# A state space layer's side work in other banks and steps, two more sums on ScalarE and GpSimd, and a convolution's first term on ScalarE

## The chip, the cores and the metric

The kernel runs on one core of a Trainium2 chip. The metric is the time of one execution on the device, in microseconds (us). A core has five engines that run their own programs side by side and meet at semaphores: TensorE (PE), VectorE (DVE), ScalarE (ACT), GpSimd (POOL) and SyncE (SP), which here only starts transfers. PE writes to PSUM, which the kernel uses as eight banks of 512 float32 per partition; ScalarE and VectorE read it.

## What is computed

Four residual layers on x (4 images, 384 channels, 48 by 48 positions). Only the first, a state space (Mamba) block, is touched by the change. The other three (a patch-wise Fourier filter, a deformable 11 by 11 depthwise convolution, a mixture of four experts) follow it in time.

```python
xs = gn(x).transpose(0, 2, 3, 1).reshape(b, L, c)          # L = 2304
xin, z = split(xs @ in_proj_w.T)                           # 768 channels each
xc = conv1d(xin, conv_w, taps=4, causal, per channel)
xin = silu(xc + conv_b)
dt, B, C = split(xin @ x_proj_w.T, [24, 16, 16])
dt = softplus(dt @ dt_proj_w.T + dt_proj_b)
for t in range(L):                                         # h: 768 x 16
    h = exp(dt[t] * A) * h + dt[t] * B[t] * xin[t]
    y[t] = sum over the 16 states of h * C[t]
y = (y + xin * D) * silu(z)
out = layernorm(y @ out_proj_w.T) * ln_gamma + ln_beta
x = x + out
```

## The kernel before

The sequence of an image (2304 positions) is cut into NQ = 6 chunks of T = 384 positions; four images give NCH = 24 chunks, `k`. A chunk is worked off in STEPS = 96 steps, `n`, that is 48 pairs of steps: 16 states, and for each three pairs of channel blocks.

The main work of a pair `p`: ACT makes two exps of dt times A (L600) and sets the start state (L605), seven steps ahead; POOL makes dt * x * B for a state, transposed, into `a_dBT` (L882); PE transposes it into the PSUM tensor `pw0` or `pw1` (`inputs`, L451, at even steps); DVE runs the recurrence as one scan over two channel blocks (L744). Then PE turns one third of the state's result into `pw2` (`turned`, L462, at odd steps), and DVE multiplies it by C and adds it to the accumulator `a_acc` (`weighed`, L763; L757 for the first state). That is a unit `u`, 48 in a chunk; the unit of pair `p` is `p - 3`. `pw2` holds one unit at a time, so `turned` waits until the unit before is read. The units in LENT (20, 22, 24, 26, 38, 41, 43) don't go to DVE: ACT copies them with the factor C to `a_tm12` (L614) and POOL adds them (L894). `lent(hh)` counts them, for the values that the semaphores `a_cw`, `p_cw`, `v_acc` are waited for.

The side work is one chunk behind or ahead. For chunk k-1 (`post_*`): skip term and gate (transposes A, L344; DVE L640; POOL L793), the output projection O (L353), layer norm (ACT L490, DVE L646, POOL L799 to L803, ACT L493), transposes G (L360), DVE L655, and the store. For chunk k+1 (`pre_*`, `gate_*`): the input projection P (L373), its copy to `a_raw` (L509), the convolution of four taps (first term on POOL, L828; three products on ACT, L521; three sums on POOL, L834), one Silu over the chunk (L524), and one over the gate (L567), the x projection X (L381), B and C turned (L387), the dt projection V (L394) with Abs and Relu (L548, L549), Exp and Ln (L552, L556) for the softplus, POOL L841 and L845, transposes T (L401) with ACT L562, and the gate projection Z (L413) with ACT L577.

The order is written by hand: each of these generators yields the step at which its next piece is due, and `march` merges them, on each engine for itself, by due time: at step `n` all pieces due by `n` come first, then the main work. PE takes side pieces at odd steps only (`odd=True`), ahead of `turned`. The due times are the tables A_AT, O_AT, LN_AT, G_AT, T_AT, Z_AT and the numbers in the yields. The engines' programs are fixed in this order, and each instruction waits for those ahead of it.

The side groups use two PSUM banks of one bank each: `ps3` (S) and `ps2` (D). `Turn.claim` keeps them in turn: a group that takes a bank waits for the semaphore with which the one before it there was read. P, the turned B and C, V, T and Z are in S; A, O, X, G and the statistics in D.

In the third chunk of an image (q = 2) the next image's group norm statistics are gathered: SP loads 18 pieces to `a_sx` (`stats`, L951), one after the other, and DVE reads each (L705). SP also loads `a_xs` for chunk k+2 (L946) and stores chunk k-1 (`store0`, L926), in one queue.

Of the kernel before, what the change touches and what calls it, by code (L numbers as in the profile page):

```python
# [323 lines left out]

# [1857 lines left out]
```

## Time and profile before

| | us |
|---|---|
| median of 3 runs | 5354.77 |
| lowest and highest | 5343.97, 5362.83 |
| the profiled execution | 5347.93 |
| its span, first to last instruction | 5346.1 |
| state space layer, scans from and to | 126.1, 3328.9 |
| an ordinary chunk | 133.0 |
| a chunk with statistics | 144.2 |

The span is that of the profiled execution; 1.8 us of its time lie around it. The times of an engine's groups of instructions are sums of their durations; where instructions overlap, start to start is shorter than the mean duration. In the timelines, the number in brackets is the idle time of the engine before the instruction and what ended it. The chunk that starts at 1055.6 us (the eighth) is taken as the ordinary one; step n of it is reached by DVE with its scan number n/2.

### The profile page before, as it was taken

What the parts mean: (1) busy time and instruction counts of PE and PEld (TensorE: products, weight loads), DVE (VectorE), ACT (ScalarE), POOL (GpSimd) and SP (SyncE); (2) the same over time, 40 slices, a digit from 0 to 9 for tenths busy, and PEclk for the clock granted to TensorE, in tenths of its full rate; (3) what the DMA queues carried; (4) which work ended last, traced back from release to release, by engine and by line L of the source; (5) the groups of instructions that cost most, each with busy time, mean ns of one, the idle gap of its engine ahead of it and who ended that gap; (6) DMA issues with size and microseconds to landing.
All of it is one profiled execution on the core that took longest, in us unless ns stands there. A gap on an engine that the chain in (4) does not pass through costs nothing.

```text
span 5346.1 us, 78656 instructions
## 1 busy us (share of the span) xinstructions
PE 4686.3 (88%) x28623; PEld 3835.5 (72%) x28623; DVE 4381.3 (82%) x4965; ACT 3070.4 (57%) x6391; POOL 2970.7 (56%) x3552
## 2 busy tenths in 40 slices
PE   4888888888888888888888886779998899999999
PEld 2666666666666666666666665446877799999999
DVE  1999999999999999999999999677677765665555
ACT  3777777777777777777777774333332223333333
POOL 3776777777777777777777775456554520000000
PEclk8999999999999999999999999889797988999999
DMA  2001000001000001000000001110201021112110
GB/s 78 1 13 33 10 10 10 10 11 35 10 10 10 10 11 35 10 10 10 10 10 10 10 5 44 44 32 20 92 20 41 26 72 53 54 51 60 45 60 29
DMA packets 96933, 148.64 MB, mean 28 GB/s; under 512 B 5748, under 2 KB 93604, under 8 KB 96548
## 3 DMA queue, kind: packets, MB, share of 16 engines
q1 hardware_dynamic: 96548, 143.63, 8.4%
q8 instruction: 227, 3.72, 0.3%
q14 instruction: 158, 1.29, 0.1%
HBM read 101.00 MB, written 42.61 MB: 27 GB/s over the span
## 4 chain that ended last, share of the span: by engine, by line
PE 50%; issue 15%; DVE 15%; POOL 12%; ACT 7%; DMA 1%; POOLq 0%; DVEq 0%; SPq 0%; ACTq 0%
PE pw L1776 8%; PE pw L1763 6%; PE pw L462 6%; PE pw L451 6%; DVE a_h L744 5%; POOL a_dBT L882 4%; PE ps L413 3%; PE ps L353 3%; DVE b_cv L1393 3%; PE ps L373 2%; DVE a_acc L763 2%; PE ps L1763 2%; POOL a_xin L834 2%; POOL a_acc L894 2%; PE pw L1176 2%
## 5 line engine op out<-in xcount | busy, mean ns | idle before, releaser
L744 DVE TENSOR_TENSOR_SCAN a_h<-a_dA,pw 128x771 f32<-128x771 f32 x1152 | 2015.7, 1752 | 125.6 <-PE pw L451 124.6
L600 ACT ACTIVATE a_dA<-a_dt,a_Aneg 128x384 f32<-128x384 f32 x2304 | 1345.5, 607 | 155.0 <-DVE a_h L744 150.1
L462 PEld LDWEIGHTS pw<-g_ident,a_h 128*128 128x128 f32 x6912 | 786.6, 142 | 619.8 <-DVE a_acc L763 267.1
L882 POOL TENSOR_SCALAR a_dBT<-a_dtxT,a_BC 128x768 f32<-128x768 f32 x1152 | 1026.2, 909 | 300.7 <-PE pw L451 216.6
L462 PE MATMUL pw<-g_ident,a_h 128*128 128x128 f32 x6912 | 983.1, 279 | 227.5 <-DVE a_acc L763 158.1
L451 PE MATMUL pw<-g_ident,a_dBT 128*128 128x128 f32 x6912 | 958.9, 276 | 4.8 <-POOL a_dBT L882 4.8
L763 DVE SCALAR_TENSOR_TENSOR a_acc<-pw,a_BC,a_acc 128x768 f32<-128x768 f32 x912 | 915.3, 1004 | 52.5 <-PE pw L462 48.1
L451 PEld LDWEIGHTS pw<-g_ident,a_dBT 128*128 128x128 f32 x6912 | 806.5, 143 | 6.5 <-POOL a_dBT L882 5.5
L834 POOL TENSOR_TENSOR a_xin<-a_xin,a_tm 128x384 f32<-128x384 f32 x432 | 433.3, 1003 | 34.2 <-ACT a_tm L521 9.0
L1887 DVE TENSOR_TENSOR d_hf<-d_hf,d_wb 128x384 f32<-128x384 f32 x288 | 159.1, 557 | 312.4 <-ACT d_hf L1819 300.2
L894 POOL TENSOR_TENSOR a_acc<-a_acc,a_tm 128x768 f32<-128x768 f32 x168 | 307.4, 1830 | 171.1 <-ACT a_tm L614 170.2
L413 PE MATMUL ps<-a_xn,a_WinT 128*128 128x384 f32 x864 | 345.5, 502 | 30.7 <-ACT a_sz L577 15.1
L373 PE MATMUL ps<-a_xn,a_WinT 128*128 128x384 f32 x864 | 350.8, 490 | 10.2 <-ACT a_raw L509 5.1
L353 PE MATMUL ps<-a_WoT,a_sz 128*128 128x384 f32 x864 | 338.9, 489 | 23.1 <-POOL a_sz L793 23.1
L1819 ACT ACTIVATE d_hf<-pw,d_b 128x384 f32<-128x384 f32 x216 | 125.2, 580 | 352.0 <-PE pw L1763 352.0
L1279 ACT ACTIVATE b_xh<-ps 128x384 fp32r<-128x384 f32 x144 | 70.6, 490 | 415.5 <-PE ps L1132 415.5
L1776 PE MATMUL pw<-e_hh,c_W2h 128*128 128x384 f32 x864 | 288.8, 334 | 1.7 <-DVE e_hl L1892 1.7
L1776 PE MATMUL pw<-e_hl,c_W2h 128*128 128x384 f32 x864 | 288.6, 334 | 0.0
L1776 PE MATMUL pw<-e_hh,c_W2l 128*128 128x384 f32 x864 | 288.6, 334 | 0.0
L1591 POOL TENSOR_SCALAR b_xw<-b_x,b_sw,b_bw 128x384 f32<-128x384 f32 x288 | 223.1, 796 | 114.8 <-PE pw L1132 114.7
L1575 POOL TENSOR_TENSOR b_cv<-b_cv,b_tm 128x768 f32<-128x768 f32 x96 | 196.3, 2045 | 131.4 <-ACT b_tm L1260 127.0
L521 ACT ACTIVATE a_tm<-a_raw,a_pv 128x384 f32<-128x384 f32 x432 | 259.5, 601 | 7.4 <-POOL a_xin L834 7.3
(228 smaller groups left out, 9377.7 us busy)
## 6 DMA issues: line engine op xcount, KB each, us to landing
d_wb<-cw SPq DMA_DIRECT2D x24, 768.0 KB, 5.7
a_xs<-in_x SPq DMA_DIRECT2D x24, 576.0 KB, 3.9
x<-a_xs SPq DMA_DIRECT2D x24, 576.0 KB, 3.0
b_x<-x SPq DMA_DIRECT2D x24, 576.0 KB, 4.4
b_xs<-x SPq DMA_DIRECT2D x24, 576.0 KB, 5.0
e_xs<-x SPq DMA_DIRECT2D x24, 576.0 KB, 3.8
out<-e_xs SPq DMA_DIRECT2D x24, 576.0 KB, 5.8
a_sx<-in_x SPq DMA_DIRECT2D x54, 192.0 KB, 2.3
```

Of the source, the lines that this page charges most:

```text
L353: t = e.matmul(pd[:, 0:C], m[f"a_sz{o}"][:, j, tb * 128:(tb + 1) * 128], m["a_WoT"][:, j, :], start=j == 0, stop=j == 5)
L373: t = e.matmul(ps[:, 0:T], m["a_WinT"][:, kk, i * 128:(i + 1) * 128], m["a_xn"][:, kk, :], start=kk == 0, stop=kk == 2)
L413: t = e.matmul(ps[:, 0:T], m["a_WinT"][:, kk, DI + i * 128:DI + (i + 1) * 128], m["a_xn"][:, kk, :], start=kk == 0, stop=kk == 2)
L451: t = e.transpose(ps[:, at:at + 128], m[f"a_dBT{g % 2}"][:, tb, (c + h) * 128:(c + h + 1) * 128], ident[:])
L462: t = e.transpose(m["pw2"][:, c * 128:(c + 1) * 128], m[f"a_h{g % 2}"][:, c // 2, first_col(c) + tb * 128:first_col(c) + (tb + 1) * 128], ...
L600: e.activation(dA[:, first_col(c):first_col(c) + T], m[f"a_dt{k % 2}"][:, c, :], ACT.Exp, scale=m["a_Aneg"][:, c, n:n + 1]).then_inc(s["a_ ...
L744: e.tensor_tensor_scan(m[f"a_h{g % 2}"][:, p % 3, :], m[f"a_dA{pi % NDA}"][:], m[f"pw{pi % 2}"][:, COL:COL + PAIR], 1.0, ALU.mult, ALU.add ...
L763: e.scalar_tensor_tensor(out=acc, in0=ps, scalar=cs, in1=acc, op0=ALU.mult, op1=ALU.add).then_inc(s["v_acc"], 1)
L834: e.tensor_tensor(xin[:, i, :], xin[:, i, :], m[f"a_tm{pr % NTM}"][:], ALU.add).then_inc(s["p_cv"], 1)
L882: t = e.tensor_scalar(m[f"a_dBT{g % 2}"][:, tb, :], m[f"a_dtxT{o}"][:, tb, :], m[f"a_BC{o}"][:, tb, n:n + 1], 1.0, ALU.mult, ALU.mult)
L1763: t = e.matmul(hidden3(m, hi), m[f"c_{A}"][:, kk, col], m[f"e_{B}{o}"][:, kk, :], start=kk == z == 0, stop=kk == z == 2)
L1776: t = e.matmul(ps, m[f"c_{A}"][:, i, col], m[f"e_{B}{u % 2}"][:, i, :], start=x == 0 and i == 0 and z == 0, stop=x == 3 and i == z == 2, s ...
```

## The change

- Units 6 and 13 (EARLY) go to ACT and POOL as well, in all chunks but those with statistics, so nine of 48 in 21 chunks. They use a new buffer, `a_tm13`, that lies over `a_sx` and `a_dt3`, with the waits that this needs.
- The first term of the convolution goes from POOL (L828) to ACT (`a_c0`), in the order first, second, third, fourth tap, for the first block second, third, first, fourth.
- V alternates between the banks S and D, T goes from S to D.
- Other due times: O and the layer norm earlier, X, B and C, V, Exp and Ln later, G from 60, 62.5, 66 to 68.1, 72.1, 76.1, Z and T other steps, Z with spacing 1.2 for 1.3.
- SP starts 16 instead of 13 of the statistics' loads ahead of the store of chunk k-1 and the load of chunk k+2.

```diff
-    m.new("a_sx", [128, T])
...
+    at = m.at
+    m.new("a_tm13", [128, DI])
+    m.section(at)
+    m.new("a_sx", [128, T])
     m.new("a_dt3", [128, T], F32R)
...
-O_AT, O_GAP, LN_AT = (18.8, 30, 40.2), (1.8, 1.6, 1.1), (29.5, 39.8, 47)
-G_AT = (60, 62.5, 66)
-T_AT = (78.6, 79.8, 81, 85.6, 86.6, 87.6)
-Z_AT = (63.5, 67.5, 71.5, 75, 82, 88.8)
+O_AT, O_GAP, LN_AT = (18.4, 29.2, 39.2), (1.8, 1.6, 1.1), (29.1, 39, 46.3)
+V_AT = (58.4, 59.5, 60.6, 61.7, 62.8, 63.9)
+G_AT = (68.1, 72.1, 76.1)
+T_AT = (80.2, 81.1, 82, 86, 86.9, 87.8)
+Z_AT = (64.8, 68.8, 72.8, 76.8, 82.8, 89.6)
+Z_GAP = 1.2
-LENT = (20, 22, 24, 26, 38, 41, 43)
+LENT, EARLY = (20, 22, 24, 26, 38, 41, 43), (6, 13)
+def has_stats(k):
+    return k % NQ == 2 and k // NQ + 1 < NB
+def lent_units(k):
+    return () if k == NCH else LENT if has_stats(k) else EARLY + LENT
...
@@ pre_pe
-        yield 47 + 1.2 * j
+        yield 47.7 + 1.2 * j
-    yield 56.8
+    yield 57.4
-        yield 58 + 0.8 * i
-        S.claim("a_v", 6 * k + i + 1)
+        yield V_AT[i]
+        (D if i % 2 else S).claim("a_v", 6 * k + i + 1)
-            S.claim("a_dtx", 6 * k + 3 * hf + tb + 1)
+            D.claim("a_dtx", 6 * k + 3 * hf + tb + 1)
@@ gate_pe
-            yield at + 1.3 * kk
+            yield at + Z_GAP * kk
@@ pre_act
-        for j in range(1, 4):
-            yield 6.2 + 5.4 * i + j
+        for j in (1, 2, 0, 3) if i == 0 else (0, 1, 2, 3):
+            yield 6.2 + 5.4 * i + 0.8 * j + (2 if i == 0 and j in (0, 3) else 0)
+            if j == 0:
+                w.wait_ge("p_sz", 6 * (k - 2) + i + 1)
+                w.wait_ge("p_dtx", 6 * (k - 1) + i + 1)
+                e.activation(m[f"a_xin{o}"][:, i, :], raw[:, i, 0:T], ACT.Identity, scale=pv[:, i, 0:1], bias=pv[:, i, 4:5]).then_inc(s["a_c0"], 1)
+                continue
-    yield 54.5
+    yield 55.2
-    yield 57.3
+    yield 57.9
-        yield 58.4 + 0.8 * i
+        yield V_AT[i] + 0.4
-    yield 64.5
+    yield 65.3
-    yield 67
+    yield 67.5
@@ gate_act
-        yield at + 3
+        yield at + 2 * Z_GAP + 0.4
@@ weighed on ACT
-        w.wait_ge("p_cv", 24 * min(k + 2, NCH))
+        if u in EARLY:
+            w.wait_ge("v_st", GN * min(k // NQ + (k % NQ > 2), NB - 1) + 18)
+            w.wait_ge("pe_V", 6 * (k + 1))
+        else:
+            w.wait_ge("p_cv", 18 * min(k + 2, NCH))
@@ pre_pool
-        yield 7.5 + 5.4 * i
...
-        e.tensor_scalar(xin[:, i, :], raw[:, i, 0:T], pv[:, i, 0:1], pv[:, i, 4:5], ALU.mult, ALU.add).then_inc(s["p_cv"], 1)
         for j in range(1, 4):
-            yield 7.5 + 5.4 * i + j
+            yield 7.5 + 5.4 * i + j + (1.5 if i == 0 else 0)
+            w.wait_ge("a_c0", 6 * k + i + 1)
@@ added on POOL
-        e.tensor_tensor(acc, acc, m["a_tm12"][:], ALU.add).then_inc(s["p_cw"], 1)
+        e.tensor_tensor(acc, acc, m["a_tm13" if u in EARLY else "a_tm12"][:], ALU.add).then_inc(s["p_cw"], 1)
@@ l0_sp
-        for i in range(more - 5):
+        for i in range(more - 2):
             stats(b + 1, i)
         if k > 0:
             store0(e, m, d, w, k - 1)
         if k + 2 < NCH:
             load(k + 2)
-        for i in range(max(0, more - 5), more):
+        for i in range(max(0, more - 2), more):
             stats(b + 1, i)
```

## Rows read from the trace of the kernel before

**Rows 1.** The page's first part: busy us of each engine, share, instructions.

```profile
PE 4686.3 (88%) x28623; PEld 3835.5 (72%) x28623; DVE 4381.3 (82%) x4965; ACT 3070.4 (57%) x6391; POOL 2970.7 (56%) x3552
```

**Rows 2.** Busy time by windows, three chunks: window, length, engines, PEclk, DMA, GB/s.

```profile
1055.60:1188.60 133.00, 116.49 (x750) 89.66 (x750) 126.31 (x107) 101.15 (x218) 101.47 (x128) 0.99 0.04 11
1467.30:1598.50 131.20, 114.82 (x750) 88.33 (x750) 126.08 (x106) 100.92 (x218) 101.22 (x127) 1.00 0.03 10
1188.60:1332.80 144.20, 120.69 (x750) 90.89 (x750) 135.08 (x130) 101.77 (x219) 101.87 (x128) 0.96 0.11 32
```

**Rows 3.** Groups of instructions by line: count, busy us, mean ns, idle before.

```profile
L763 DVE SCALAR_TENSOR_TENSOR a_acc<-pw,a_BC,a_acc 128x768 f32<-128x768 f32 x912 | 915.3, 1004 | 52.5 <-PE pw L462 48.1
...
L894 POOL TENSOR_TENSOR a_acc<-a_acc,a_tm 128x768 f32<-128x768 f32 x168 | 307.4, 1830 | 171.1 <-ACT a_tm L614 170.2
...
L614 ACT ACTIVATE a_tm<-pw,a_BC 128x768 f32<-128x768 f32 x168 | 151.2, 900 | 129.1 <-PE pw L462 129.1
...
L828 POOL TENSOR_SCALAR a_xin<-a_raw,a_pv 128x384 f32<-128x384 f32 x144 | 95.0, 660 | 30.4 <-ACT a_raw L509 25.7 <-POOL a_sz L793 4.6
```

**Rows 4.** Timeline of DVE, ordinary chunk: start, us, line; two scans in a row last.

```profile
1081.95 1.75 DVE L744 TENSOR_TENSOR_SCAN a_h<-a_dA,pw 128x771 f32<-128x771 f32 x1
...
1084.82 1.75 DVE L744 TENSOR_TENSOR_SCAN a_h<-a_dA,pw 128x771 f32<-128x771 f32 x1
...
1087.42 1.75 DVE L744 TENSOR_TENSOR_SCAN a_h<-a_dA,pw 128x771 f32<-128x771 f32 x1
...
1106.28 1.75 DVE L744 TENSOR_TENSOR_SCAN a_h<-a_dA,pw 128x771 f32<-128x771 f32 x1
...
1137.84 3.51 DVE L744 TENSOR_TENSOR_SCAN a_h<-a_dA,pw 128x771 f32<-128x771 f32 x2
```

**Rows 5.** Timeline of PE, ordinary chunk, steps 19 to 21.

```profile
1082.31 0.88 PE L353 MATMUL ps<-a_WoT,a_sz 128*128 128x384 f32 x2 [1.14 <-POOL a_sz L793]
1083.03 0.82 PE L462 MATMUL pw<-g_ident,a_h 128*128 128x128 f32 x6
...
1085.63 0.82 PE L462 MATMUL pw<-g_ident,a_h 128*128 128x128 f32 x6
```

**Rows 6.** Timeline of ACT, ordinary chunk, at step 34.

```profile
1102.09 0.49 ACT L509 ACTIVATE a_raw<-ps 128x384 f32<-128x384 f32 x1 [0.65 <-PE ps L373]
1103.04 0.71 ACT L493 ACTIVATE a_ob<-a_ob,a_lsc 128x384 f32<-128x384 f32 x1 [0.46 <-POOL a_lsc L803]
```

**Rows 7.** Timeline of all engines, ordinary chunk, Silu and steps 46 to 48.

```profile
1111.00 2.13 ACT L524 ACTIVATE a_xin<-a_xin 128x2304 f32<-128x2304 f32 x1
...
1121.51 0.91 PE L381 MATMUL ps<-a_xin,a_WxT 128*128 128x384 f32 x2 [2.00 <-ACT a_ob L490]
...
1124.81 1.76 DVE L744 TENSOR_TENSOR_SCAN a_h<-a_dA,pw 128x771 f32<-128x771 f32 x1 [2.54 <-PE pw L451]
```

**Rows 8.** The same, the dt matmuls, step 61.

```profile
1137.81 0.45 PE L394 MATMUL ps<-a_dt,a_Wdt 128*128 128x384 f32 x1 [1.14 <-ACT a_raw L549]
```

**Rows 9.** The same, from the x copy to the Ln, and step 90.

```profile
1131.86 0.47 ACT L532 ACTIVATE a_dt<-ps 128x384 fp32r<-128x384 f32 x1
...
1150.60 0.49 ACT L577 ACTIVATE a_sz<-ps 128x384 f32<-128x384 f32 x1
1150.98 2.21 ACT L556 ACTIVATE a_dt<-a_dt,a_one 128x2304 f32<-128x2304 f32 x1
...
1181.69 1.76 DVE L744 TENSOR_TENSOR_SCAN a_h<-a_dA,pw 128x771 f32<-128x771 f32 x1 [1.10 <-PE pw L451]
```

**Rows 10.** Timelines of SP and DVE in a chunk with statistics.

```profile
1286.51 0.38 SPq L926 DMA_DIRECT2D x<-a_xs  x1
...
1294.06 0.56 DVE L705 BATCH_NORM_STATS2 a_bn<-a_sx 128x6 f32<-128x384 f32 x1 [4.08 <-DMA a_sx<-in_x]
...
1304.95 1.02 DVE L763 SCALAR_TENSOR_TENSOR a_acc<-pw,a_BC,a_acc 128x768 f32<-128x768 f32 x1 [2.58 <-PE pw L462]
```

**Rows 11.** Busy time by windows, the stretch at low clock in the ordinary chunk.

```profile
1122.50:1125.90 3.40, 3.40 (x15) 2.69 (x14) 1.09 (x1) 2.37 (x5) 2.30 (x4) 0.50 0.02 5
```

More of the change, by code:

```diff
@@ L311, with is_lent @@
 A_AT = (6.2, 8, 9.8, 11.6, 13.4, 15.2)
-O_AT, O_GAP, LN_AT = (18.8, 30, 40.2), (1.8, 1.6, 1.1), (29.5, 39.8, 47)
-G_AT = (60, 62.5, 66)
-T_AT = (78.6, 79.8, 81, 85.6, 86.6, 87.6)
-Z_AT = (63.5, 67.5, 71.5, 75, 82, 88.8)
-LENT = (20, 22, 24, 26, 38, 41, 43)
+O_AT, O_GAP, LN_AT = (18.4, 29.2, 39.2), (1.8, 1.6, 1.1), (29.1, 39, 46.3)
[9 more added lines that the diff above has]
+    return () if k == NCH else LENT if has_stats(k) else EARLY + LENT
+def is_lent(hh):
+    return hh >= 0 and hh % PAIRS in lent_units(hh // PAIRS)
 def lent(hh):
-    k, u = divmod(hh, STEPS // 2)
-    return len(LENT) * k + sum(x < u for x in LENT)
+    k, u = divmod(hh, PAIRS)
+    return sum(len(lent_units(i)) for i in range(k)) + sum(x < u for x in lent_units(k))
 def chunk(k):
@@ L389, in pre_pe @@
     for i in range(6):
-        yield 58 + 0.8 * i
-        S.claim("a_v", 6 * k + i + 1)
+        yield V_AT[i]
+        (D if i % 2 else S).claim("a_v", 6 * k + i + 1)
         w.wait_ge("v_dt3", k + 1)
         w.wait_ge("v_w", 7)
-        e.matmul(ps[:, 0:T], m["a_Wdt3"][:, i * 128:(i + 1) * 128], m["a_dt3"][:], start=True, stop=True).then_inc(s["pe_V"], 1)
+        e.matmul((pd if i % 2 else ps)[:, 0:T], m["a_Wdt3"][:, i * 128:(i + 1) * 128], m["a_dt3"][:], start=True, stop=True).then_inc(s["pe_V"], 1)
     for hf in range(2):
@@ L456, in turned @@
         w.wait_ge("v_scan", 3 * g + 3)
-        if hh > 0 and (hh - 1) % PAIRS in LENT:
+        if is_lent(hh - 1):
             w.wait_ge("a_cw", lent(hh))
@@ L531, in pre_act @@
     w.wait_ge("pe_BC", k)
+    if k > 0:
+        w.wait_ge("p_cw", lent(PAIRS * (k - 1) + EARLY[-1] + 1))
     e.activation(m["a_dt3"][:], pd[:, 0:T], ACT.Copy).then_inc(s["a_x"], 1)
     e.activation(m["a_tm0"][32:64, :], pd[32:64, 0:T], ACT.Copy).then_inc(s["a_x"], 1)
-    yield 57.3
+    yield 57.9
     w.wait_ge("pe_BC", k + 1)
@@ L547, in pre_act @@
         w.wait_ge("a_exp", 3 * PAIRS * (k - 1))
-        e.activation(dt[:, i, :], ps[:, 0:T], ACT.Abs, bias=pv[:, i, 5:6])
-        e.activation(raw[:, i, 3:T + 3], ps[:, 0:T], ACT.Relu, bias=pv[:, i, 5:6]).then_inc(s["a_v"], 1)
-    yield 64.5
+        pi = pd if i % 2 else ps
+        e.activation(dt[:, i, :], pi[:, 0:T], ACT.Abs, bias=pv[:, i, 5:6])
+        e.activation(raw[:, i, 3:T + 3], pi[:, 0:T], ACT.Relu, bias=pv[:, i, 5:6]).then_inc(s["a_v"], 1)
+    yield 65.3
     w.wait_ge("a_v", 6 * (k + 1))
     e.activation(dt[:], dt[:], ACT.Exp, scale=-1.0).then_inc(s["a_sp"], 1)
-    yield 67
+    yield 67.5
     w.wait_ge("a_sp", 2 * k + 1)
@@ L561, in pre_act @@
         hf, tb = divmod(u, 3)
-        e.activation(m[f"a_dtxT{o}"][:, tb, hf * T:(hf + 1) * T], ps[:, 0:T], ACT.Copy).then_inc(s["a_dtx"], 1)
+        e.activation(m[f"a_dtxT{o}"][:, tb, hf * T:(hf + 1) * T], pd[:, 0:T], ACT.Copy).then_inc(s["a_dtx"], 1)
 def silu_gate(e, m, w, k):
@@ L623, in main @@
         def main(n):
-            if n % 2 == 0 and n // 2 - TB - 1 in LENT:
+            if n % 2 == 0 and n // 2 - TB - 1 in lent_units(k):
                 weighed(k, n // 2 - TB - 1)
@@ L660, in pre_dve @@
     s, ps, dt3 = m.s, m["ps2"], m["a_dt3"]
-    yield 55.3
+    yield 56
     w.wait_ge("pe_X", k + 1)
@@ L809, in halo_pool @@
     w.wait_ge("a_pr", 18 * k)
+    w.wait_ge("a_c0", 6 * k)
     if k % NQ == 0:
@@ L912, in main @@
         def main(n):
-            if n % 2 and (n - 3) // 2 - TB in LENT:
+            if n % 2 and (n - 3) // 2 - TB in lent_units(k):
                 added(k, (n - 3) // 2 - TB)
@@ L950, in stats @@
         w.wait_ge("v_st", GN * (b - 1) + 18 if i == 0 else GN * b + i)
+        w.wait_ge("p_cw", lent(PAIRS * (NQ * (b - 1) + 2)))
         e.dma_start(m["a_sx"][:], xv[b, :, c, q * T:(q + 1) * T]).then_inc(s["d_sx"], 16)
```

29 lines of the change are left out of this document (12 added, 17 removed).

## The prediction

> **What bounds the kernel now.** I read the busy times first, then the time by chunk, then the order of instructions inside one chunk. Over the whole span TensorE (PE) is busy 88% and VectorE (DVE) 82% [rows 1]. The change touches only the state space layer, 24 chunks that start between 126 and 3206 us. An ordinary chunk takes 133.0 us; DVE is busy for 126.3 of them, ScalarE (ACT) for 101.2, GpSimd (POOL) for 101.5 [rows 2]. A chunk in which the statistics of the next image are gathered takes 144.2 us with the TensorE clock at 0.96, and one whose clock never fell takes 131.2 us [rows 2].
>
> A DVE busy for 95% looks like the bound. It is only half of it. In the stretch of steps 19 to 38 a pair of steps takes 2.60 us on DVE, scan to scan [rows 4]. PE takes 2.60 us there too, from one turned sum to the next (1083.03 to 1085.63): six transposes of state, six of inputs, one projection matmul and one output matmul, 0.65 us each, no idle time between them; the first and the last are shown [rows 5]. Two engines run at the same pace, and work taken from one of them shortens nothing. Elsewhere DVE waits for PE: 2.54 us where the x projection begins, 1.10 at step 90; in the dt matmuls PE waits for each eviction [rows 7, 8, 9].
>
> **How I count.** Pair by pair, from those durations. A pair costs PE 1.30 us of transposes plus its side groups (0.65 for a 384-column matmul of two passes, 0.33 for three transposes). A turned sum may start once the sum before it is read, and DVE wants it 1.66 us later, at the end of its scan (a scan of 1.75 us, less the overlap); it takes PE 0.82 [rows 4, 5]. So PE may be 0.8 us late for nothing, and 2.60 - 1.30 = 1.3 us of side work a pair keep it from falling further behind. What goes beyond that, DVE waits for.
>
> **Part 1: two more units to ACT and POOL (6 and 13).** 21 chunks have them: not the three with statistics. A unit is a weighted sum of 1.00 us on DVE; ACT's copy takes 0.90 [rows 3]. What DVE gives up is less than the row's mean, since instructions overlap: two scans in a row take 3.51 us, so a pair without a sum takes 1.75 and the gain is 2.60 - 1.75 = 0.85 us, 1.7 for both [rows 4]. Both lie inside the PE-paced stretch.
> Unit 6 is turned at step 19. There PE waits until POOL has the last gated product: 1.14 us [rows 5]. POOL loses 2 x 0.66 us of convolution before it [rows 3], but must now wait for the third product from DVE, so I let it finish 0.3 us earlier. Yet the output matmul, due at 18.8 behind a projection matmul at 18.7, is now due at 18.4, before it, so 0.65 us of work falls behind the wait. PE leaves step 19 0.3 us later, and the unit gains nothing.
> Unit 13 is turned at step 33. ACT's program has, before that copy, the copy of the last projection, whose matmul stands in that same step of PE: then 0.5 us for it, 0.5 for the new first term, 0.6 for a layer norm scaling, 0.5 for a product [rows 3, 6]. The copy starts 2.1 us after ACT gets its first input, and PE's next turned sum waits about 1.4 us. The output matmuls also move forward: three instead of two groups in step 31, the first behind an ACT copy that now has a first term ahead of it, 0.4 us.
> Added up for steps 18 to 36: 24.3 us before (scans at 1081.95 and 1106.28, [rows 4]), 26.4 after, **+2.0 us** where the skipped sums promise -1.7: PE falls back 0.3 us at step 19, 0.4 at 31 and 1.4 at 33, and since PE paces these pairs, the two sums bring nothing.
>
> **Part 2: the first term of the convolution.** POOL loses 6 x 0.66 us and gains 2 x 1.83; ACT gains 6 x 0.5 and 2 x 0.9 [rows 3]. ACT idles 32 us of 133, most of it in steps 6 to 36 waiting for PE [rows 2, 6], which hides its 4.8. If that cover were gone, it would cost at most those 4.8 us a chunk. But the second added unit holds POOL's last convolution sums until the ACT copy is there, so Silu starts 3.2 us later than before (1111.0 [rows 7]), 1.2 us later against the scans.
>
> **Part 3: the other steps.** Before, the x projection waits until 1121.51 for an ACT copy and DVE's scan sits idle 2.54 us; PE then runs at clock 0.50 for 3.4 us [rows 7, 11]. A chunk without that drop is 1.8 us shorter (133.0 - 131.2 [rows 2]). After, the projection is due one pair later and the copy one exp sooner, but Silu is late. I get waits of 0.8 us for the layer norm statistics and 0.5 for a turned sum, in place of 3.2 (the 2.54, the sum before that waits too, and its aftermath): **-1.9 us** over steps 36 to 50, with no drop of the clock there.
> The dt matmuls alternate between two banks, which ends the wait of 1.14 us for each eviction [rows 8]. What is late next is ACT: a matmul pair every 2.6 us needs 1.9 us of Abs and Relu beside 1.1 us of exps, and at step 60 the lent copy 26 now stands behind a dt eviction whose matmul is in PE's step 61. Waits of 1.2, 0.6 and 0.2 us remain where, with the end of the x projection, about 2.6 stood. Steps 50 to 68: **-0.6 us**, besides 1.6 us of layer output work (G) that only moves to steps 69 to 77.
> Then a new wait. The first gate group's copy was due at 66.5, before the Ln at 67 (1150.60 and 1150.98, [rows 9]). It is now due at 67.6, behind the Ln at 67.5. The second gate group starts in the same step of PE (69) in which the first ends, and needs that copy. From the x copy (1131.86) to the Ln ACT took 19.1 us; I find 18.5 after, plus 2.2 for the Ln and 0.4 for the copy. PE comes to the second group 18.2 us after the x copy and stands for 2.9 us; with the 0.8 us by which a turned sum may be late, DVE loses 2.2. Steps 68 to 80: **+1.9**.
> At steps 80 to 96 the gate group starts one step earlier among the turned dtx groups, and these have their own bank: 1.10 us [rows 9] goes, about 0.6 comes back after unit 38. **-0.5**.
>
> **Part 4: the queue of SP.** In a statistics chunk the load for step 70 stands behind a store that waits for G, and a load of the next chunk; DVE waits 4.08 us and 2.58 more when the clock has fallen [rows 10], 7.2 with two small ones. After, three more loads go ahead of the store. The last two follow it; the store waits for a G ten steps later. From the store's release to that load's landing took 7.5 us (1286.51 to 1294.06); its user at step 84 comes about 8.5 us after. Hidden, with one microsecond to spare; without it, up to 2 us in three chunks. Such a chunk: 144.2 - 7.2 + about 0.9 for the new waits, **-6.3 us**.
>
> **The sum.** An ordinary chunk: 133.0 + 2.0 - 1.9 - 0.6 + 1.9 - 0.5 = 133.9. A standstill of 2.9 us of PE is longer than that ahead of [rows 11], so the clock may fall after it; I give half the chunks that, at 1.7 us: 134.7. Sixteen chunks gain 1.7 in length, three (which had no drop) 3.5: +38. Statistics chunks: -19. Chunk 0 and chunk 23, with little beside the scans: -1.0 and -1.7. The prologue: six terms of 0.66 and five waits of 1.14 less [rows 3, 8], -8. Together +8 us: 5347.9 + 8 = 5356. The profiled run lies 6.8 us under the median of the three, so the same in the median is 5363; I say **5360**.
>
> **What the Trainium skill says.** Its page Perfetto Trace Analysis (Matmuls) wants independent groups to rotate through banks so that an eviction overlaps the next group. The dt rows show such waits; the gate groups stay in one bank. The same page (Identifying the Most-Contended Engine) would take the engine of highest occupancy first, here DVE. By that rule the freed DVE time shows in full, the first rival; rows 5 speak against it.
>
> **Rivals.** *A, DVE paces and the new waits stay away (0.34).* If ACT reaches step 68 early enough and unit 13's copy on time, an ordinary chunk is 133.9 - 2.2 - 1.3 = 130.4 and keeps the clock. Sixteen times -2.6, three times -0.9, less 30 for the rest: 5347.9 - 74 = 5274; with only one of the two waits gone about 5305. For it: DVE's 126.3 of 133; against: the same-step orders above.
> *B, the wait behind the Ln costs the clock in every chunk (0.28).* It decides if a standstill of 2.9 us brings the clock down wherever it falls; before, 2.0 us did so in most chunks, not in all [rows 2, 7]. Then 133.9 + 1.7 = 135.6: 16 x 2.6 + 3 x 4.4 - 30 = +25, in the median 5380; with a late load or a missed exp besides, 5395.
> *C, the steps don't change what runs (0.03):* several new due times round to the same step. Then only part 4 and the prologue count, about 5328.
> *Forecast (0.35):* gains and new waits cancel, 5340 to 5370.
> A measurement of this kernel can tell about 0.3% (16 us) from no change. Faster by more: most of A and C, 0.36. Slower: B and a little of the forecast, 0.31. Same: 0.33. The range takes half of A and all but the end of B: 5272 to 5392.
>
> **What would show it.** Timeline of an ordinary chunk: the gate matmul group waiting for its own eviction for about 3 us near step 69, the copy right behind the Ln; the turned sum after unit 13 waiting for ACT; pairs 9 to 17 at 26 us; no wait at the x projection above 1 us; statistics chunks near 138 without DVE waiting for a DMA. If pairs 9 to 17 take 23 us, or ACT is at the Ln when PE is at step 67, the forecast is wrong and A holds.

## The result, and the profile after

The changed kernel takes 5413.97 us (median of 4 runs, 5410.99 to 5418.08); the kernel before, on the same chip, 5358.80 (now the median of 4 runs, 5343.97 to 5365.40). The ratio is 1.0107, with a 95% interval of 1.0089 to 1.0126: slower by 55 us. The prediction said 5360, with 5392 as the upper end. The profiled execution took 5418.08 us, the slowest of the four, with a span of 5416.3.

The page's first part, then three groups of instructions (count, busy us, mean ns, idle time before and what ended it), of the changed kernel. Its lines are numbered anew: the scan is L775 (before L744), the weighed sum L794 (L763), turned L481 (L462), inputs L470 (L451), ACT's copy for a unit L645 (L614), O L372, P L392, Z L432, Ln L583.

```profile
PE 4714.4 (87%) x28623; PEld 3841.1 (71%) x28623; DVE 4347.5 (80%) x4923; ACT 3168.1 (58%) x6577; POOL 2954.5 (55%) x3450
...
L775 DVE TENSOR_TENSOR_SCAN a_h<-a_dA,pw 128x771 f32<-128x771 f32 x1152 | 2013.4, 1751 | 108.2 <-PE pw L470 107.2
...
L794 DVE SCALAR_TENSOR_TENSOR a_acc<-pw,a_BC,a_acc 128x768 f32<-128x768 f32 x870 | 872.6, 1003 | 181.2 <-PE pw L481 181.0
...
L413 PE MATMUL ps<-a_dt,a_Wdt 128*128 128x384 f32 x144 | 51.9, 413 | 9.9 <-ACT a_BC L564 8.2 <-ACT a_raw L576 1.7
```

Two groups of the kernel before that [rows 3] don't hold, the scans and the dt matmuls:

```profile
L744 DVE TENSOR_TENSOR_SCAN a_h<-a_dA,pw 128x771 f32<-128x771 f32 x1152 | 2015.7, 1752 | 125.6 <-PE pw L451 124.6
...
L394 PE MATMUL ps<-a_dt,a_Wdt 128*128 128x384 f32 x144 | 64.5, 448 | 77.8 <-ACT a_raw L549 77.4 <-ACT a_BC L538 0.3
```

DVE has 34 us less to do [rows 1], and waits for PE 111 us longer: 108.2 + 181.2 against 125.6 + 52.5 [rows 3] in scans and sums. PE has the same 28623 instructions and is busy 28 us longer, 15 of them behind the last scan. So the 42 sums were taken away, and DVE, rid of 34 us of work, waits more than that for PE.

By windows (window, length, busy us of PE, PE's weight loads, DVE, ACT, POOL, then granted clock, DMA, GB/s): chunk 0, an ordinary chunk whose clock never fell, one where it did, one with statistics.

```profile
116.80:242.00 125.20, 102.18 (x669) 78.17 (x667) 115.08 (x85) 100.98 (x218) 90.59 (x105) 0.98 0.00 1
932.30:1067.90 135.60, 116.02 (x750) 88.26 (x750) 124.44 (x105) 105.35 (x227) 101.14 (x123) 1.00 0.03 10
1067.90:1204.90 137.00, 117.48 (x750) 89.62 (x750) 124.47 (x105) 105.31 (x227) 101.21 (x123) 0.99 0.03 10
1204.90:1343.60 138.70, 116.55 (x750) 88.00 (x750) 134.52 (x129) 104.43 (x225) 98.12 (x123) 1.00 0.12 35
```

Against [rows 2] the ordinary chunk grew from 133.0 to 137.0 and the statistics chunk fell from 144.2 to 138.7. Summed over chunks: 16 ordinary ones +64.2, the three after a statistics chunk (134.5 before, 138.9 to 140.7 now) +16.8, statistics -14.6, chunk 0 +4.5, chunk 23 -0.6, prologue -9.4: +61 us. The other 9 us between the two profiled executions lie behind the last scan, nearly all in layers that the change doesn't touch; the clock was at 0.50 there for 316 us, and for 287 before.

Where in the chunk? The table gives the time in us from scan to scan in the eighth chunk of each kernel, by pairs (pair p is steps 2p and 2p+1); the runs are introduced below. The clock fell in this chunk of before (at step 46), changed, e1, e4, e5 and e10 (step 70) and e8 (step 19), and not in the others.

| kernel | 0-8 | 9-17 | 18-24 | 25-33 | 34-39 | 40-47 | chunk |
|---|---|---|---|---|---|---|---|
| before | 26.33 | 24.33 | 21.40 | 25.32 | 15.80 | 19.77 | 132.96 |
| changed | 26.32 | 27.02 | 19.49 | 23.47 | 20.40 | 20.31 | 137.01 |
| e1_no_early | 26.33 | 26.12 | 19.03 | 23.46 | 20.39 | 20.29 | 135.63 |
| e2_copy_first | 26.33 | 26.99 | 19.48 | 23.46 | 17.03 | 20.30 | 133.59 |
| e3_units_only | 26.33 | 25.09 | 21.11 | 24.96 | 15.80 | 19.78 | 133.08 |
| e4_o_behind_p | 26.32 | 26.33 | 19.46 | 23.46 | 20.40 | 20.30 | 136.27 |
| e5_steps_only | 26.32 | 25.61 | 19.04 | 23.46 | 20.38 | 20.30 | 135.12 |
| e7_mended | 26.33 | 24.25 | 18.44 | 23.47 | 17.03 | 19.93 | 129.44 |
| e8_units_3_5 | 25.07 | 28.76 | 18.44 | 23.46 | 17.02 | 19.93 | 132.69 |
| e9_units_3_5_own_wait | 25.06 | 25.49 | 18.43 | 23.47 | 17.03 | 19.93 | 129.43 |
| e10_after_own_wait | 26.33 | 25.60 | 19.49 | 23.46 | 20.40 | 20.30 | 135.58 |
| e12_mended_own_wait | 26.32 | 23.70 | 18.44 | 23.46 | 17.02 | 19.93 | 128.88 |
| e13_unit_5 | 25.42 | 23.86 | 18.45 | 23.46 | 17.02 | 19.92 | 128.13 |

The layer output work (G), 1.56 us of DVE, is in column 25-33 before and in 34-39 wherever the new steps are kept.

Three places carry most of the loss; a fourth, at step 86, is shown further below. Timelines of the changed kernel (start, us, engine, line, then the idle time before). First step 19, the window after scan 9:

```profile
1094.52 0.88 PE L372 MATMUL ps<-a_WoT,a_sz 128*128 128x384 f32 x2 [1.74 <-POOL a_sz L824]
1095.24 0.81 PE L392 MATMUL ps<-a_xn,a_WinT 128*128 128x384 f32 x2
1095.88 0.82 PE L481 MATMUL pw<-g_ident,a_h 128*128 128x128 f32 x6
```

PE leaves the wait 26.64 us after the chunk's first scan, before it was 26.69 [rows 5]: POOL's last gated product is hardly earlier. But the projection matmul (L392) now comes behind the wait, not ahead of it. Second, step 33, the copy of unit 13:

```profile
1116.20 0.49 ACT L528 ACTIVATE a_raw<-ps 128x384 f32<-128x384 f32 x1 [1.30 <-PE ps L392]
1116.72 0.71 ACT L538 ACTIVATE a_xin<-a_raw,a_pv 128x384 f32<-128x384 f32 x1
1117.34 0.69 ACT L512 ACTIVATE a_ob<-a_ob,a_lsc 128x384 f32<-128x384 f32 x1
1117.94 0.60 ACT L545 ACTIVATE a_tm<-a_raw,a_pv 128x384 f32<-128x384 f32 x1
1118.44 0.88 ACT L645 ACTIVATE a_tm<-pw,a_BC 128x768 f32<-128x768 f32 x1
...
1119.38 0.88 PE L481 MATMUL pw<-g_ident,a_h 128*128 128x128 f32 x6 [1.26 <-ACT a_tm L645]
```

ACT isn't idle before the copy (L645): it stands behind four operations of side work. PE has turned the unit into `pw2` and can't turn the next one until it is copied. Third, steps 68 to 70:

```profile
1164.01 2.26 ACT L583 ACTIVATE a_dt<-a_dt,a_one 128x2304 f32<-128x2304 f32 x1
...
1166.12 0.54 ACT L604 ACTIVATE a_sz<-ps 128x384 f32<-128x384 f32 x1
...
1166.71 1.45 PE L432 MATMUL ps<-a_xn,a_WinT 128*128 128x384 f32 x2 [2.40 <-ACT a_sz L604]
...
1169.48 1.02 DVE L794 SCALAR_TENSOR_TENSOR a_acc<-pw,a_BC,a_acc 128x768 f32<-128x768 f32 x1 [3.04 <-PE pw L481]
```

The gate group's copy (L604) is right behind the Ln, PE stands 2.40 us, and then two matmuls take 1.45 us, where the two of the projection above (L392) take 0.81: the clock is down.

### The profile page after: what moved, and what is told of

Same layout as the page of the kernel before. It is cut to its first block, busy times and chain, and to the rows that moved or that the text cites. A ratio compares the mean times of both kernels' runs of the same rounds, so it can differ in the third digit from the quotient of the medians.

```text
span 5416.3 us, 78678 instructions
## 1 busy us (share of the span) xinstructions
PE 4714.4 (87%) x28623; PEld 3841.1 (71%) x28623; DVE 4347.5 (80%) x4923; ACT 3168.1 (58%) x6577; POOL 2954.5 (55%) x3450
## 4 chain that ended last, share of the span: by engine, by line
PE 41%; DVE 19%; issue 16%; ACT 13%; POOL 10%; SPq 0%; DMA 0%; DVEq 0%; POOLq 0%; ACTq 0%
DVE a_h L775 9%; PE pw L1803 8%; PE pw L1790 6%; PE pw L481 5%; ACT a_dA L627 4%; POOL a_xin L860 4%; DVE a_acc L794 3%; PE pw L470 3%; PE ps L432 3%; DVE b_cv L1420 3%; PE ps L1790 2%; POOL a_sz L824 2%; PE pw L1203 2%; PE ps L1203 2%; PE pw L1117 2%
## 5 line engine op out<-in xcount | busy, mean ns | idle before, releaser
L775 DVE TENSOR_TENSOR_SCAN a_h<-a_dA,pw 128x771 f32<-128x771 f32 x1152 | 2013.4, 1751 | 108.2 <-PE pw L470 107.2
L481 PEld LDWEIGHTS pw<-g_ident,a_h 128*128 128x128 f32 x6912 | 780.3, 142 | 712.4 <-DVE a_acc L794 278.2
L481 PE MATMUL pw<-g_ident,a_h 128*128 128x128 f32 x6912 | 988.8, 280 | 291.0 <-DVE a_acc L794 136.7
L794 DVE SCALAR_TENSOR_TENSOR a_acc<-pw,a_BC,a_acc 128x768 f32<-128x768 f32 x870 | 872.6, 1003 | 181.2 <-PE pw L481 181.0
L470 PE MATMUL pw<-g_ident,a_dBT 128*128 128x128 f32 x6912 | 953.4, 275 | 4.8 <-POOL a_dBT L908 4.8
L470 PEld LDWEIGHTS pw<-g_ident,a_dBT 128*128 128x128 f32 x6912 | 802.6, 143 | 6.6 <-POOL a_dBT L908 5.5
L920 POOL TENSOR_TENSOR a_acc<-a_acc,a_tm 128x768 f32<-128x768 f32 x210 | 383.9, 1828 | 190.4 <-ACT a_tm L645 190.4
L432 PE MATMUL ps<-a_xn,a_WinT 128*128 128x384 f32 x864 | 369.9, 518 | 93.6 <-ACT a_sz L604 70.3
L372 PE MATMUL ps<-a_WoT,a_sz 128*128 128x384 f32 x864 | 340.9, 491 | 43.8 <-POOL a_sz L824 35.3
L392 PE MATMUL ps<-a_xn,a_WinT 128*128 128x384 f32 x864 | 350.4, 490 | 9.5 <-POOL a_xn L881 5.1
```

What stands on the lines that cost most here:

```text
L392: t = e.matmul(ps[:, 0:T], m["a_WinT"][:, kk, i * 128:(i + 1) * 128], m["a_xn"][:, kk, :], start=kk == 0, stop=kk == 2)
L432: t = e.matmul(ps[:, 0:T], m["a_WinT"][:, kk, DI + i * 128:DI + (i + 1) * 128], m["a_xn"][:, kk, :], start=kk == 0, stop=kk == 2)
L470: t = e.transpose(ps[:, at:at + 128], m[f"a_dBT{g % 2}"][:, tb, (c + h) * 128:(c + h + 1) * 128], ident[:])
L481: t = e.transpose(m["pw2"][:, c * 128:(c + 1) * 128], m[f"a_h{g % 2}"][:, c // 2, first_col(c) + tb * 128:first_col(c) + (tb + 1) * 128], ...
L775: e.tensor_tensor_scan(m[f"a_h{g % 2}"][:, p % 3, :], m[f"a_dA{pi % NDA}"][:], m[f"pw{pi % 2}"][:, COL:COL + PAIR], 1.0, ALU.mult, ALU.add ...
L794: e.scalar_tensor_tensor(out=acc, in0=ps, scalar=cs, in1=acc, op0=ALU.mult, op1=ALU.add).then_inc(s["v_acc"], 1)
```

## The experiments

Ratios are against the kernel before, run beside each group, with 95% intervals; the changed kernel is at 1.0107. The median of before was 5350.64 beside e1 to e4, 5357.58 beside e5 to e8, 5363.06 beside e9 to e12 and 5347.11 beside e13, so the ratios compare better than the times. Lengths of chunks and falls of the clock are counted in the profiled execution of each kernel.

| run | us | ratio |
|---|---|---|
| e1_no_early | 5373.41 | 1.0042 (1.0027 to 1.0057) |
| e2_copy_first | 5341.15 | 0.9984 (0.9975 to 0.9993) |
| e3_units_only | 5359.79 | 1.0016 (1.0006 to 1.0025) |
| e4_o_behind_p | 5394.63 | 1.0083 (1.0068 to 1.0098) |
| e5_steps_only | 5372.61 | 1.0030 (1.0016 to 1.0044) |
| e6_loads_only | 5326.16 | 0.9952 (0.9933 to 0.9972) |
| e7_mended | 5262.20 | 0.9834 (0.9798 to 0.9869) |
| e8_units_3_5 | 5318.98 | 0.9936 (0.9916 to 0.9956) |
| e9_units_3_5_own_wait | 5262.15 | 0.9829 (0.9797 to 0.9861) |
| e10_after_own_wait | 5373.16 | 1.0033 (1.0018 to 1.0048) |
| e12_mended_own_wait | 5254.65 | 0.9813 (0.9786 to 0.9839) |
| e13_unit_5 | 5236.89 | 0.9791 (0.9773 to 0.9810) |

**The copy behind the Ln.**

The only edit to the changed kernel (e2_copy_first) is the due time of the Ln:

```diff
-    yield 67.5
+    yield 67.7
```

> The changed kernel with one due time altered: the Ln at step 67.7 instead of 67.5, so that ACT copies the first gate group (due 67.6) before the Ln. If the same-step order of copy and Ln makes PE's standstill of 2.40 us and the fall of the clock that follows in 15 of 19 ordinary chunks, both go: 3.0 us of waiting less on DVE at that sum and 1.4 us of slow clock, part of it taken by what is late next (the exp behind the Ln); 2.5 to 4.5 us a chunk in some 22 chunks, 5315 to 5360 us. Rival, the wait only moves (ACT is late by itself and the Ln or an exp behind it becomes the wait): the time within 10 us of 5414.

The time falls by 1.2% of the kernel before, 66 us, as the theory has it; the clock falls twice in the layer instead of 20 times. The same steps in this kernel, where PE's wait before the second gate group is 0.28 us:

```profile
1142.71 0.52 ACT L604 ACTIVATE a_sz<-ps 128x384 f32<-128x384 f32 x1
1143.10 2.24 ACT L583 ACTIVATE a_dt<-a_dt,a_one 128x2304 f32<-128x2304 f32 x1
1143.29 0.91 PE L432 MATMUL ps<-a_xn,a_WinT 128*128 128x384 f32 x2 [0.28 <-ACT a_sz L604]
```

Pairs 34 to 39 lose 3.37 us: 1.96 of waiting and 1.41 of slow clock (a changed chunk without the fall has 18.99 there). Nothing else is late in its place: DVE has no wait above 0.06 us in these pairs. One due time was worth more than the whole loss of the change.

**The added units.** Units 6 and 13 back to DVE, all else as changed:

```diff
-LENT, EARLY = (20, 22, 24, 26, 38, 41, 43), (6, 13)
+LENT, EARLY = (20, 22, 24, 26, 38, 41, 43), ()
```

With them goes a wait of ACT's x copy for GpSimd's sum of the last added unit, here as in e7 and e12. In the changed kernel that copy is always released by PE, so the wait held nothing up.

> The changed kernel without the two added units (6 and 13 go to DVE again), all else kept. Its pairs 9 to 17 took 27.0 us against 24.3 before. If the two units cost there by where their copies stand in ACT's program and by the convolution sums that they hold up, the stretch comes back to about 24.8 us (the rest is the first term's, through the wait for the gated product), the x projection is early again and an ordinary chunk takes about 134.5 us after 137.0: 5360 us, 50 us below the changed kernel. Rival, PE paces there whatever the units do: the stretch stays near 27 and the time within 10 us of 5414. Rival, DVE is what counts: two sums of 0.85 us more in 21 chunks, 5440 us. The wait behind the Ln stays 2.4 us in all three.

It got faster by 0.65%, 35 us, though DVE has 42 sums more; some 11 us of it are the clock, which fell 12 times instead of 20. The rivals with DVE or PE alone as the pace fall. But the stretch came back only to 26.12, not to 24.8: the units cost 0.9 us of its 2.7. Pairs 9 and 10 are 6.03 without and 6.07 with unit 6, so that unit is worth nothing; pair 17 takes 2.58 without and 3.72 with unit 13, which pair 16 gives back 0.28 of.

**The output matmul ahead of the projection.**

```diff
-O_AT, O_GAP, LN_AT = (18.4, 29.2, 39.2), (1.8, 1.6, 1.1), (29.1, 39, 46.3)
+O_AT, O_GAP, LN_AT = (18.8, 29.2, 39.2), (1.8, 1.6, 1.1), (29.1, 39, 46.3)
```

> The changed kernel with the first output matmul due at 18.8 instead of 18.4, so that it stands behind the projection matmul of that step as before. The prediction held that 0.65 us of projection fell behind the 1.14 us wait for the last gated product (measured 1.74 us in the changed kernel). If so, that wait falls to about 1.1 and pairs 9 to 17 lose 0.65 us: 0.4 to 0.65 us a chunk, 5400 to 5405 us. Rival, the wait for POOL decides when PE leaves that step whatever stands ahead: within 5 us of 5414.

Pairs 9 to 17 lose 0.69 us, the chunk 0.7 (137.0 to 136.3), the time 13 us by the ratios. The place of that matmul is the cause of that part.

**Parts alone.** e3_units_only is the kernel before with the units and the first term; e5_steps_only is the kernel before with the steps, banks and loads.

> The kernel before in all its steps, banks and loads, with the two added units and the first term of the convolution on ACT. By the prediction's count these two parts cost 2.0 us a chunk in pairs 9 to 17 (measured with all parts together: 2.7), less the 0.4 us that the earlier output matmuls were to cost, and make the x projection, which DVE already waited 2.54 us for, later by 1 to 2 us. 2.5 to 4 us a chunk in 20 chunks, less 4 us in the prologue: 5400 to 5430 us. Rival, DVE paces and the new steps are what costs: 1.7 us a chunk less than before, about 5325 us. Rival, the loss needs the two together: no change, within 15 us of the kernel before.

> The kernel before with only the new steps, banks and loads: no added units, the convolution's first term on GpSimd as before. Against the run that had the first term on ScalarE and no added units (5373 us, ordinary chunks 134.2 without and 135.6 with the fall of the clock, pairs 9 to 17 in 26.1): if the first term costs nothing in the chunks, their lengths are the same, and the prologue is 8 us longer: 5381 us. Rival, the first term on ScalarE costs where ScalarE's chain is late (the wait for the gated product at step 19, Silu): pairs 9 to 17 come to 25.5 or less, and the time to 5365.

e3 is a miss: 9 us slower than before, not 50. The time alone would fit the third rival, that the loss needs the two parts together; the chunks don't. In the old steps the two parts cost 0.76 us in pairs 9 to 17, and the late Silu 1.0 in pairs 18 to 24 (21.11 against 20.09 in a chunk of before whose clock didn't fall). At equal clock the chunk is 1.8 us longer (133.1 against 131.3). But the clock, which fell in 13 of the 16 ordinary chunks before, fell in none here, and that gave nearly all of it back. It stayed up although PE stands longer before the x projection, 3.03 us where it was 2.00:

```profile
1124.48 0.91 PE L400 MATMUL ps<-a_xin,a_WxT 128*128 128x384 f32 x2 [3.03 <-ACT a_ob L509]
```

Why is open.

e5 fits the rival in the chunks: with the first term on POOL pairs 9 to 17 take 25.61, not 26.12. In the time that hardly shows (1.0030 against 1.0042, with intervals that overlap); the first scan starts 3.4 us later. The 2.69 us of that stretch are then: steps 1.28 (25.61 - 24.33), first term 0.51 (26.12 - 25.61), units 0.90 (27.02 - 26.12).

**The loads alone.**

```diff
-        for i in range(more - 5):
+        for i in range(more - 2):
```

> The kernel before with only the order of the queue of SP changed: 16 instead of 13 loads of the statistics ahead of the store. The prediction takes 7.2 us off each of three statistics chunks: from 144.1 to about 137, 21 us in all, 5330 us, nothing else changed. Rival, the last two loads behind the store now wait for it (it still waits for the layer output at step 60 to 66, so this would have to be another stretch): the chunk falls by less than 4 us, 5340 us or more.

The statistics chunk of this kernel, by windows:

```profile
1182.74:1318.95 136.21, 116.75 (x750) 87.65 (x750) 134.38 (x129) 101.93 (x219) 101.66 (x129) 1.00 0.12 34
```

144.2 to 136.2, three times nearly 8 us, and 31 us in the medians. This one line was the best part of the change. About 10 of the 31 us are the clock, which fell in 9 instead of 13 ordinary chunks of the profiled execution, and in one instead of three of those after a statistics chunk.

**The mended kernel.** The changed one with no added units (and without their wait), the Ln at 67.7, and these tables:

```diff
-O_AT, O_GAP, LN_AT = (18.4, 29.2, 39.2), (1.8, 1.6, 1.1), (29.1, 39, 46.3)
-T_AT = (80.2, 81.1, 82, 86, 86.9, 87.8)
-Z_AT = (64.8, 68.8, 72.8, 76.8, 82.8, 89.6)
+O_AT, O_GAP, LN_AT = (18.8, 30, 39.2), (1.8, 1.6, 1.1), (29.5, 39.8, 46.3)
+T_AT = (78.6, 79.8, 81, 85.6, 86.6, 87.6)
+Z_AT = (64.8, 68.8, 72.8, 76.8, 82, 88.8)
```

> The changed kernel with every step undone that the traces show to cost: no added units, the Ln behind the first gate copy, the output projection's first two groups and their layer norm steps as before (18.8, 30; 29.5, 39.8), the turned dtx groups and the last two gate groups at the steps of before but in the new banks. If the costs add by stretch: pairs 0 to 8 26.3, 9 to 17 24.4, 18 to 24 19.1, 25 to 33 23.5, 34 to 39 17.0, 40 to 47 19.0 to 19.8, in all 129.5 to 130 us for an ordinary chunk that took 133.0 before, statistics chunks 135, no fall of the clock: 5255 to 5275 us. Rival, a mended stretch only passes the lateness on to the next one (the x projection, the gate copies): above 5300.

```profile
1023.18:1152.62 129.44, 115.03 (x750) 88.15 (x750) 125.89 (x107) 103.76 (x224) 97.62 (x122) 1.00 0.03 10
1152.62:1288.84 136.22, 116.98 (x750) 87.59 (x750) 134.42 (x130) 104.76 (x225) 98.02 (x123) 1.00 0.12 36
```

An ordinary chunk takes 129.44 us after 132.96, and the kernel is 1.7% faster than before. The costs add by stretch, which is what a sum assumes. (The statistics chunk was expected at 135 and took 136.2.) DVE is busy for 125.9 us here, 1.4 more than in the changed kernel, and the chunk is 7.6 us shorter.

**Where a sum is worth something.** The mended kernel with units 3 and 5:

> The mended kernel with two added units again, but 3 and 5 instead of 6 and 13: these are turned in pairs 6 and 8, where the trace shows TensorE ready 0.4 us before it is asked and VectorE without idle time. If a sum that is taken from VectorE is worth its 0.85 us only where VectorE alone paces, both show here: 1.2 to 1.7 us off pairs 0 to 8 and 25 to 35 us off the mended kernel's time. Rival, it is worth nothing anywhere, since TensorE's total is the bound: within 8 us of the mended kernel.

Another miss: 57 us slower than the mended kernel, about half of it the clock (a chunk without its fall takes 131.03, most 132.7). The gain is there, 1.26 us in pairs 0 to 8, but pair 9 takes 6.77 us:

```profile
1063.64 1.80 POOL L920 TENSOR_TENSOR a_acc<-a_acc,a_tm 128x768 f32<-128x768 f32 x1
...
1065.53 0.90 ACT L645 ACTIVATE a_tm<-pw,a_BC 128x768 f32<-128x768 f32 x1 [0.96 <-POOL a_acc L920]
1066.36 0.99 POOL L824 TENSOR_TENSOR a_sz<-a_xin,a_sz 128x384 f32<-128x384 f32 x1
...
1067.49 1.06 PE L372 MATMUL ps<-a_WoT,a_sz 128*128 128x384 f32 x2 [2.98 <-POOL a_sz L824]
```

POOL's sum for unit 3 stands ahead of its last gated product, and the first output matmul waits for all six products. It reads only one of them. So the next three runs let each output matmul wait for its own:

```diff
             if j == 0:
                 D.claim("a_ob", 3 * k + tb + 1)
-                w.wait_ge("p_sz", 6 * (k + 1))
                 w.wait_ge("d_w0", 96)
+            w.wait_ge("p_sz", 6 * k + j + 1)
```

> The mended kernel with the added units 3 and 5, and with each output matmul waiting for its own block's gated product instead of the first one waiting for all six. With these units before, pairs 0 to 8 took 1.3 us less, and pair 9 lost 4 us, since GpSimd's last product came 1.57 us later behind the added sum and TensorE stood for it. If that wait is the whole loss, it is gone: 1.3 us a chunk off the mended kernel's 129.45 us, 5230 to 5240 us. Rival, GpSimd itself is now late for what follows (convolution, Silu, the next input products): the loss moves to pairs 18 to 24 and the time stays above 5262.

> The changed kernel with the same change of waits and nothing else. In it TensorE stands 1.74 us at step 19 for the last gated product, and pairs 9 and 10 take 6.04 us with one sum skipped. If that wait is why unit 6 brings nothing, the two pairs fall to about 4.5 us, the wait behind unit 13 stays (pair 17, 3.7 us) and may grow: 1.0 to 1.6 us a chunk, 5380 to 5390 us. Rival, the side groups pace step 19 anyway: less than 0.5 us a chunk, above 5400.

> The mended kernel (no added units) with the same change of waits. Its pair 9 takes 2.78 instead of 2.58 us and pairs 10 to 13 run at TensorE's 2.60 with turned sums 0.81 us behind the scan. If TensorE's lateness comes from the wait at step 19 alone, these pairs fall to 2.58: 0.2 to 0.5 us a chunk, 5250 to 5258 us. Rival, six transposes of state, six of inputs and two side matmuls fill 2.60 us whatever came before: no change beyond 0.2 us a chunk, 5258 to 5265.

e10: in the changed kernel pairs 9 and 10 fall from 6.07 to 4.65 us; two pairs of e12 take 5.16, so unit 6 is worth 0.5 at last. The wait behind unit 13 stays (pair 17, 3.71). The time falls by 0.7%, more than expected: some 11 us are the clock, which fell 12 times in the layer instead of 20. e12: 0.56 us a chunk, all of it in pairs 9 to 17, most of which now run at DVE's 2.58 us. e9 is a miss: no gain over e7. The wait for the product is gone, and behind it stood a second one:

```profile
1048.46 1.81 POOL L920 TENSOR_TENSOR a_acc<-a_acc,a_tm 128x768 f32<-128x768 f32 x1
1050.36 0.90 ACT L645 ACTIVATE a_tm<-pw,a_BC 128x768 f32<-128x768 f32 x1 [0.98 <-POOL a_acc L920]
1051.41 0.84 PE L481 MATMUL pw<-g_ident,a_h 128*128 128x128 f32 x6 [1.44 <-ACT a_tm L645]
```

Both units share one buffer: ACT's copy of unit 5 waits for POOL's sum of unit 3. (It stood in e8's rows as well.) With unit 5 alone:

> The mended kernel with its own wait for each output matmul and one added unit, 5. Units 3 and 5 together gave 0.35 and 0.91 us in pairs 6 and 8, and lost 1.45 us at pair 9, where ScalarE's copy of unit 5 stood 0.98 us for GpSimd's sum of unit 3, since both use one buffer. Unit 5 alone has the buffer free. Theory: where VectorE alone paces, a sum taken from it is worth its 0.85 to 0.91 us, less 0.2 that comes back as TensorE is less far ahead: 0.6 to 0.8 us a chunk in 21 chunks, 12 to 17 us below the 5254.65 of the mended kernel with own waits, 5238 to 5243. Rival, what pair 8 gains is waited for at step 19 by some other engine: within 4 us of 5254.65.

```profile
1016.55:1144.68 128.13, 114.79 (x750) 88.14 (x750) 124.71 (x106) 104.63 (x225) 99.17 (x123) 1.00 0.03 10
```

0.75 us a chunk less than e12, and 14.8 us from the first scan to the last, as expected; pair 8 took 1.67 us instead of 2.58. (The medians lie 18 us apart, but they come from two chips; the ratios differ by 0.22%, 12 us.) This kernel is 2.1% faster than the one before.

## Why the prediction was wrong

Right were the mechanisms, the two new waits, and in sum what the wait behind the Ln costs together with the clock. The step that failed most is the one for steps 80 to 96: it was to give 0.5 us a chunk and cost 0.5 to 2.7. The 19 chunks that are neither the first nor the last nor have statistics took some 43 us more than forecast: 24 in steps 80 to 96, 12 in part 1, 5 in steps 36 to 68 and 1 in steps 68 to 80 with the clock. So the gains that were to cancel the new waits weren't there.

- **What bounds it.** That PE and DVE pace together holds: 42 sums were taken from DVE and the kernel got slower by them (e1). That PE is held only by its own work in pairs 9 to 17 does not: without the wait at step 19 the pairs run at 2.58 us (e12). The Trainium skill, Perfetto Trace Analysis (Identifying the Most-Contended Engine), goes for the engine of highest occupancy first, here DVE. A sum less on DVE was worth nothing (unit 6), -0.9 us (unit 13) or +0.75 us (unit 5), by its place.
- **Part 1, +2.0 us: measured +2.69.** Step 19 was forecast at 0.3 and cost 0.61 (pairs 9 and 10, 5.46 to 6.07). The mechanism is the one named. The mis-sized term is POOL, which was to be 0.3 us earlier and was 0.05. Step 31 was forecast at 0.4 and cost 0.96 (pairs 15 and 16, 5.38 to 6.34), of it 0.58 the first term ahead of ACT's copy (pair 15, 2.79 in e5, 3.37 in e1). The first term was priced at 0.5 us on ACT and takes 0.71. Unit 13: 1.4 forecast, 1.12 measured.
- **Part 3, steps 36 to 50: -1.9, measured -1.91.** Of it 1.31 is the clock: a chunk of before in which it stayed up has 20.09 in pairs 18 to 24, not 21.40. The wait at the x projection fell to 0.61 us.
- **Steps 50 to 68: -0.6, measured nothing.** The columns give 25.32 - 1.56 - 23.47 = 0.3, but a chunk of before whose clock stayed up has 24.96 there, so that the steps and the second bank gained nothing at equal clock. The waits of the list are there, one of them as PE sees it (changed kernel):

```profile
1154.13 0.85 PE L481 MATMUL pw<-g_ident,a_h 128*128 128x128 f32 x6 [1.85 <-ACT a_tm L645]
```

- **The wait behind the Ln: +1.9 without the clock.** e2 gives 1.96; against the kernel before, steps 68 to 80 grew by 1.63 where the clock stayed up (18.99 - 1.56 - 15.80). Found before the run, by reading same-step orders: 67.6 behind 67.5.
- **The clock.** Half the chunks were given its fall; 17 of 22 standstills had it, at 1.4 us rather than 1.7. Rival B (0.28), a fall in every chunk at 5380 to 5395, was nearer in the time, but that is luck in part: what the number lacked lies mostly in other steps.
- **Steps 80 to 96: -0.5, measured +0.54.** This step has the wrong sign. DVE's wait of 1.10 for the turned dtx group went, but it waits 0.80 and 1.03 us elsewhere in these pairs:

```profile
1189.71 1.76 DVE L775 TENSOR_TENSOR_SCAN a_h<-a_dA,pw 128x771 f32<-128x771 f32 x1 [0.80 <-PE pw L470]
...
1195.07 1.02 DVE L794 SCALAR_TENSOR_TENSOR a_acc<-pw,a_BC,a_acc 128x768 f32<-128x768 f32 x1 [1.03 <-PE pw L481]
```

  The last gate group's matmuls now mix with the dtx groups: ACT's copy of the fourth one comes behind the gate copy and an exp (the changed kernel's timeline):

```profile
1192.31 0.49 ACT L604 ACTIVATE a_sz<-ps 128x384 f32<-128x384 f32 x1 [1.25 <-PE ps L432]
...
1193.30 0.48 ACT L589 ACTIVATE a_dtxT<-ps 128x384 f32<-128x384 f32 x1
...
1193.83 0.55 PE L420 MATMUL ps<-g_ident,a_raw 128*128 128x128 f32 x3 [1.23 <-ACT a_dtxT L589]
```

  With the old steps in the new banks (e7) the stretch takes 19.93, before 19.77: the steps cost 0.38 of the 0.54. What the bank alone does was not tried. In the three chunks after a statistics chunk the same stretch grew from 21.3 to 22.3 and, in two of them, where the clock fell once more, 24.0. The prediction counted them as ordinary; they grew by 4.8 us more than three ordinary chunks.
- **Chunk 0: -1.0, measured +4.5.** It was said to have little beside the scans. It has the gate groups and the Ln, so it has the wait: e2 takes 3.5 us off it. Chunk 23: -1.7, measured -0.6; DVE has a new wait of 0.91 there for a layer norm copy.
- **Statistics chunks: -6.3, measured -5.3, -5.4 and -3.9.** The loads are worth 7.8 to 8.0 (e6), where 7.2 was said; the new waits in the same chunk take 2.5 back (136.2 to 138.7), where 0.9 was forecast.
- **The sum:** +8 forecast, +61 in layer 0. Of the 53 us between them the 19 chunks that were forecast at 38 and took 81 give 43, chunks 0 and 23 give 6.5, the statistics 4.3, and the prologue, forecast at -8, takes 1.4 off. An error of 1 us in a chunk's steps came 19 times.

The V groups in two banks did what the Trainium skill, Perfetto Trace Analysis (Matmuls), says of rotating banks: PE's idle time before them is 9.9 us in all against 77.8. The trace agrees on the wait. But the chunk gained nothing in steps 50 to 68 (above), where PE now stands 1.85 us for a copy of ACT, which evicts these groups as well. The banks weren't tried without the new steps.

## What to carry over

Work taken from an engine is worth its time only in stretches where that engine alone is late; read the margins pair by pair and put it there, and check what the engine that takes it over has queued behind, and with which buffer. In programs ordered by hand, write out the order inside each step where two due times meet: two orders, decided by 0.1 and 0.3 of a step, cost 66 and 13 us here, more than the whole change lost. And look at what a wait asks for: the first output matmul waited for six blocks and read one. When a gain is read from a stretch, compare chunks with the same clock: the 0.3 us that the dt matmuls seemed to give was the aftermath of a fall elsewhere.
